# Cross-attention and ternary FFN: a third plane of keys, fewer TensorE waits, maxima written in place, another order of small transfers

## What is computed

```python
x = x + xattn(layernorm(x), ctx, mask)        # x 32x56x128, ctx 32x1500x128, 16 heads of 8
#   scores = q k^T / sqrt(8), -1e9 where mask == 0, softmax over 1500 keys, times v, times Wo + bo
x = x + ffn(layernorm(x))                      # 128 -> 512 -> 128
#   weights ternary, rows quantised to 8 bits before each product, exact gelu between
```

## Time and profile before

| | |
|---|---|
| median of 3 runs | 975.32 us (970.74 to 975.33) |
| the profiled execution | 970.35 us, its span 968.6 us |
| granted TensorE clock, mean | 0.959 of full speed |

### The profile page before, as it was taken

One profiled execution on the slowest core, in us unless ns is written; L12 is line 12 of the kernel. 1 busy time (PEld: TensorE's weight loads), 2 busy tenths in 40 slices (PEclk: granted clock), 3 DMA queues, 4 the chain that ended last, 5 costly groups with the idle time before them and its releaser, 6 DMA issues.

```text
span 968.6 us, 35820 instructions
## 1 busy us (share of the span) xinstructions
PE 859.6 (89%) x12492; PEld 655.2 (68%) x12492; DVE 758.8 (78%) x2597; ACT 707.5 (73%) x1272; POOL 252.2 (26%) x262
## 2 busy tenths in 40 slices
PE   3667989999898989999898999899898989989893
PEld 2344767767676767767686777677676767767672
DVE  4578579888787979888787979788686978878754
ACT  3434658879697868879697878779596877969562
POOL 8220242222222222222222222222222222312200
PEclk9677999999999999999999999999899999999997
DMA  5540223333322333333332333333323333340100
GB/s 139 117 119 18 63 51 86 89 92 83 100 72 75 82 87 84 90 92 83 94 78 73 81 90 86 82 91 83 97 56 82 76 89 91 85 104 24 36 3 6
DMA packets 79099, 75.79 MB, mean 78 GB/s; under 512 B 10240, under 2 KB 75248, under 8 KB 78960
## 3 DMA queue, kind: packets, MB, share of 16 engines
q1 hardware_dynamic: 77167, 72.78, 29.5%
q10 hardware_dynamic: 1793, 0.83, 0.3%
HBM read 47.97 MB, written 0.92 MB: 50 GB/s over the span
## 4 chain that ended last, share of the span: by engine, by line
PE 70%; issue 12%; ACT 6%; DVE 4%; SPq 4%; DMA 2%; POOL 2%; ACTq 0%; POOLq 0%; DVEq 0%
PE ps_p L885 18%; PE ps_v L929 12%; PE ps_p L867 9%; PE ps_p L812 8%; PE ps_p L808 8%; PE ps_p L893 7%; PE ps_p L805 4%; SPq L456 2%; ACT L690 2%; ACT L723 2%; DMA ctx_sb<-in_ctx_dram 1%; DVE max_junk L1165 1%; ACT probs L723 1%; PE ps_p L836 1%; PE ps_p L832 1%
## 5 line engine op out<-in xcount | busy, mean ns | idle before, releaser
L1165 DVE CUSTOM_DVE_ANT_0 max_junk<-ps_p,mask_bias 120x500 bf16<-120x500 f32 x768 | 483.2, 674 | 71.8 <-PE ps_p L867 53.7
L723 ACT ACTIVATE probs<-ps_p 125x448 f32<-125x448 f32 x768 | 355.3, 558 | 77.1 <-PE ps_p L893 73.3
L885 PE MATMUL ps_p<-qry_hi,keys 64*125 64x224 f32 x1536 | 208.0, 291 | 6.6 <-ACT probs L723 0.6
L634 POOL TENSOR_TENSOR k_lo<-k_full,keys 128x500 fp32r<-128x500 f32 x96 | 125.7, 1316 | 319.5 <-ACT keys L713 255.6
L885 PE MATMUL ps_p<-qry_lo,keys 64*125 64x224 f32 x1536 | 192.9, 271 | 0.0
L885 PEld LDWEIGHTS ps_p<-qry_hi,keys 64*125 64x125 f32 x1536 | 150.4, 186 | 61.9 <-ACT probs L723 29.2
L867 PE MATMUL ps_p<-keys,qry_hi 64*120 64x500 f32 x768 | 161.2, 438 | 13.1 <-DMA keys<-k_lo 5.9
L929 PEld LDWEIGHTS ps_v<-probs,vals 125*32 125x32 f32 x6144 | 145.1, 110 | 23.3 <-issue 12.8
L929 PE MATMUL ps_v<-probs,vals 125*32 125x112 f32 x6144 | 160.6, 260 | 0.2 <-ACT probs L723 0.2
L893 PE MATMUL ps_p<-own_query,mask_bias 57*125 57x448 f32 x768 | 147.0, 373 | 9.3 <-DMA own_query<-shift 9.2
L885 PEld LDWEIGHTS ps_p<-qry_lo,keys 64*125 64x125 f32 x1536 | 151.1, 187 | 3.2
(11 more groups left out here) (124 smaller groups left out, 804.3 us busy)
## 6 DMA issues: line engine op xcount, KB each, us to landing
keys<-k_lo SPq DMA_DIRECT2D x384, 62.5 KB, 2.0
ctx_sb<-in_ctx_dram SPq DMA_DIRECT2D x31, 750.0 KB
mask_sb<-in_mask_Bx1xSxS_ik_dram SPq DMA_DIRECT2D x64, 328.1 KB
own_query<-shift SPq DMA_DIRECT2D x64, 1.8 KB
out_dram<-x_rows SPq DMA_DIRECT2D x16, 56.0 KB, 1.6
ctx_sb<-in_ctx_dram ACTq DMA_DIRECT2D x1, 750.0 KB
x_rows<-in_x_dram SPq DMA_DIRECT2D x1, 672.0 KB, 11.0
w_sb<-in_L_ffn_w_dram SPq DMA_DIRECT2D x2, 256.0 KB, 8.4
```

Of the source, the lines that this page charges most:

```text
L634: pool.tensor_tensor(k_lo[:, (p + n) % 2, :], k_full[:, (p + n) % 2, :], keys[:, p, 0, at].bitcast(F32), ALU.subtract)\
L723: act.activation(probs[:, (c + NG * p) % NP, h], ps_p[0:KC, BANK[how]["S", c, h], 0:HC], ACT.Exp)\
L885: pe.matmul(score_bank(c, h, how)[:, heads, :], keys[rows, p, g, at], query[rows], start=(g == 0 and part == 0), stop=False, skip_group_ch ...
L1165: dve.tensor_tensor_reduce(max_junk[0:MROWS, BANK[how][slot], :], ps_p[0:MROWS, BANK[how][slot], 0:SEG], mask_bias[0:MROWS, p, s * SEG:(s ...
```

## The change

1. `keys` has a third plane. Plane 0 is left as it is made, the high parts of all eight heads of a half in their natural rows; planes 1 and 2 are the stacked ones of before. ScalarE writes planes 0 and 1, and a new GpSimd copy of 128x500 per segment writes plane 2 from plane 0; the low parts go into planes 1 and 2. Of the four transfers of a segment, the two into plane 2 wait for that copy. The maxima read planes 1 and 2.
2. In `products`, the queries' low parts meet plane 0 in one matmul of 448 columns per half; the high parts meet planes 1 and 2 in two of 224 each. Eight matmuls become six, with the same number of columns in all.
3. TensorE leaves out a wait where an earlier one of the same step on the same semaphore asked for as much (`wait_once`; a slot's second bank is waited for first), and some waits whose condition another wait implies. The wait on `wo_rows` moves ahead of the steps.
4. The maxima's unused sums are written over the bank that they are read from, 32-bit words in PSUM; `max_junk` goes.
5. `vals` shares the ones between two neighbouring pairs of heads (values, ones, values); the rows of `wo_rows` and `den_of_row` follow.
6. In odd steps SyncE places the shift row ahead of segment 1.

```diff
-        keys = sb("keys", [D, 2, 2, SK], F32R)
+        keys = sb("keys", [D, 2, 3, SK], F32R)
         k_lo = sb("k_lo", [D, 2, SEG], F32R)
         mask_bias = sb("mask_bias", [128, 2, SK], F32R)
-        vals = sb("vals", [KC, 2, NC, NV, 2, VH])
...
-        max_junk = sb("max_junk", [128, NBANK, SEG], BF16)
...
-            def place_low(bt, n):
+            def place_keys(bt, n):
 
                 b, k, p = bt
                 made = NSEG * b + n + 1
                 at = slice(n * SEG, (n + 1) * SEG)
-                sp.wait_ge(k_lo_ready, made if isinstance(b, int) else sp.snap(made))
-                for h in range(2):
-                    for g in range(2):
+                made = made if isinstance(b, int) else sp.snap(made)
+                sp.wait_ge(k_lo_ready, made)
+                for g in range(2):
+                    if g == 1:
+                        sp.wait_ge(keys_copied, made)
+                    for h in range(2):
                         src, dst = SLOT * h + GR * g, SLOT * h + GR * (1 - g)
-                        sp.dma_start(keys[dst:dst + GR, p, g, at].bitcast(F32), k_lo[src:src + GR, (p + n) % 2, :].bitcast(F32))\
-                            .then_inc(k_lo_placed[p][n], 16)
+                        sp.dma_start(keys[dst:dst + GR, p, 1 + g, at].bitcast(F32),
+                                     k_lo[src:src + GR, (p + n) % 2, :].bitcast(F32)).then_inc(keys_placed[p][n], 16)
 
             def store(bt):
...
                     if loop or b > 1:
                         store(bt)
                     if loop or b + 2 < B:
-                        place_low(later(bt, 2), 0)
-                    if loop or b + 2 < B:
-                        place_low(later(bt, 2), 1)
+                        place_keys(later(bt, 2), 0)
                     if loop or b + 1 < B:
                         place_shift(later(bt, 1))
                     if loop or b + 2 < B:
-                        place_low(later(bt, 2), 2)
+                        place_keys(later(bt, 2), 1)
+                    if loop or b + 2 < B:
+                        place_keys(later(bt, 2), 2)
 
...
                 if n == 2:
-                    pool.wait_ge(k_lo_placed[p][0], 64 * (k + 1))
+                    pool.wait_ge(keys_placed[p][0], 64 * (k + 1))
                 else:
-                    wait(pool, k_lo_placed[1 - p][n + 1], 64 * (k + p))
+                    wait(pool, keys_placed[1 - p][n + 1], 64 * (k + p))
                 pool.tensor_tensor(k_lo[:, (p + n) % 2, :], k_full[:, (p + n) % 2, :],
                                    keys[:, p, 0, at].bitcast(F32), ALU.subtract)\
                     .then_inc(k_lo_ready, 1)
+                pool.tensor_copy(keys[:, p, 2, at], keys[:, p, 0, at].bitcast(F32)).then_inc(keys_copied, 1)
...
-                    act.activation(vals[:, p, 4 * n:4 * n + 4, :, 0, :].rearrange("p c v r -> p (c v) r"),
-                                   bank[0:KC, :].rearrange("p (v r) -> p v r", r=VH), ACT.Copy)\
+                    act.activation(vals[:, p, 4 * n:4 * n + 4, :, 0::2, :].rearrange("p c v a r -> p (c v) a r"),
+                                   bank[0:KC, :].rearrange("p (v a r) -> p v a r", a=2, r=VH), ACT.Copy)\
...
-                act.activation(keys[:, p, :, at],
+                act.activation(keys[:, p, 0:2, at],
...
+            waited = {}
+
+            def wait_once(semaphore, count, st):
+
+                level = count((st[2], 0, st[2]))
+                if level > waited.get(semaphore.name, -10 ** 9):
+                    waited[semaphore.name] = level
+                    wait(pe, semaphore, count(st))
+
+            def wait_bank(slot, how, st):
+                last, ago = before(how, slot)
+                if last is not None:
+                    wait_once(left_bank[last[0]], lambda bt: number(last, later(bt, -ago)), st)
+
+            def wait_banks(kind, n, how, st):
+
+                for h in (1, 0):
+                    wait_bank((kind, n, h), how, st)
 
...
                 if kind == "D":
                     pe.wait_ge(pv_taken, b + 1)
-                    pe.wait_ge(halves_known, 1)
+                    if isinstance(b, int):
+                        pe.wait_ge(halves_known, 1)
                 if kind == "B":
                     pe.wait_ge(wo_scaled, 1)
                 if kind == "O":
                     pe.wait_ge(attn_ready, 2 * (t + 1))
-                    pe.wait_ge(wo_rows_loaded, 16 * N_WO_ROWS)
...
                 if r == 0:
-                    pe.wait_ge(k_lo_placed[p][s], 64 * (k + 1))
-                for h in range(2):
-                    wait_bank_free(pe, ("M", n, h), how, st)
+                    pe.wait_ge(keys_placed[p][s], 64 * (k + 1))
+                wait_banks("M", n, how, st)
                 for h in range(2):
                     rows = slice(SLOT * h, SLOT * (h + 1))
                     pe.matmul(ps_p[0:MROWS, BANK[how]["M", n, h], 0:SEG],
                               qry_hi[rows, p, 2 * r:2 * r + 2, :].rearrange("p a q -> p (a q)")[:, 0:MROWS],
-                              keys[rows, p, r // 2, s * SEG:(s + 1) * SEG], start=True, stop=True)\
+                              keys[rows, p, 1 + r // 2, s * SEG:(s + 1) * SEG], start=True, stop=True)\
                         .then_inc(bank_full[BANK[how]["M", n, h]], 1)
...
                 at = slice(c * KC, (c + 1) * KC)
+                for h in range(2):
+                    rows = slice(SLOT * h, SLOT * (h + 1))
+                    pe.matmul(score_bank(c, h, how), keys[rows, p, 0, at], qry_lo[rows, p, :, :], start=True, stop=False,
+                              skip_group_check=True)
                 for g in range(2):
                     heads = slice(GH * g, GH * (g + 1))
-                    for part, query in enumerate((qry_hi[:, p, heads, 0:SQ], qry_lo[:, p, heads, :])):
-                        for h in range(2):
-                            rows = slice(SLOT * h, SLOT * (h + 1))
-                            pe.matmul(score_bank(c, h, how)[:, heads, :], keys[rows, p, g, at], query[rows],
-                                      start=(g == 0 and part == 0), stop=False,
-                                      skip_group_check=True)
+                    for h in range(2):
+                        rows = slice(SLOT * h, SLOT * (h + 1))
+                        pe.matmul(score_bank(c, h, how)[:, heads, :], keys[rows, p, 1 + g, at],
+                                  qry_hi[rows, p, heads, 0:SQ], start=False, stop=False, skip_group_check=True)
 
             def shifts(bt, c, how):
...
                 if c == 0:
                     pe.wait_ge(q_step, 4 * (b + 1))
-                if c % NG == 0:
-                    pe.wait_ge(k_lo_placed[p][c // NG], 64 * (k + 1))
-                for h in range(2):
-                    wait_bank_free(pe, ("S", c, h), how, bt)
+                wait_banks("S", c, how, bt)
                 products(bt, c, how)
...
-                if c % NG == 0:
-                    pe.wait_ge(mask_biased, NSEG * b + c // NG + 1)
                 shifts(bt, c, how).then_inc(scores_ready, 1)
+
+            def with_ones(p, c, t):
+
+                return vals[:, p, c, t // 2, t % 2:t % 2 + 2, :].rearrange("p a r -> p (a r)")
 
             def values(bt, n):
 
                 b, k, p = bt
                 if n == 0:
                     wait(pe, pv_taken, b)
-                pe.wait_ge(vals_ready, NSEG * b + n + 1)
-                pe.wait_ge(exp_done, 2 * (NC * b + NG * (n + 1)))
+                wait_once(exp_done, lambda at: 2 * (NC * at[0] + NG * (n + 1)), bt)
...
 
             step(batch(-1, 0), "open")
             step(batch(-1, 1), "lead")
+            pe.wait_ge(wo_rows_loaded, 16 * N_WO_ROWS)
             steps(pe, step)
             step(batch(B // 2, 0), "tail")
...
-                dve.tensor_tensor_reduce(max_junk[0:MROWS, BANK[how][slot], :],
+                dve.tensor_tensor_reduce(ps_p[0:MROWS, BANK[how][slot], 0:SEG],
                                          ps_p[0:MROWS, BANK[how][slot], 0:SEG],
                                          mask_bias[0:MROWS, p, s * SEG:(s + 1) * SEG].bitcast(F32), 1.0, LOWEST,
                                          ALU.add, ALU.max, seg_max[0:MROWS, 4 * h + r, s:s + 1])\
```

More of the change, by code:

```diff
@@ L309, in xattn_ffn @@
         k_hi_ready = sem("k_hi_ready")
+        keys_copied = sem("keys_copied")
         k_lo_ready = sem("k_lo_ready")
-        k_lo_placed = [[sem(f"k_lo_placed{p}_{n}") for n in range(NSEG)] for p in range(2)]
+        keys_placed = [[sem(f"keys_placed{p}_{n}") for n in range(NSEG)] for p in range(2)]
         vals_ready = sem("vals_ready")
@@ L517, in _ @@
             for n in range(NSEG):
-                place_low(batch(0, 0), n)
+                place_keys(batch(0, 0), n)
             sp.dma_start(wo_sb[:], wo).then_inc(wo_loaded, 16)
@@ L526, in _ @@
                     at = VH * (4 * t + g)
```

(13 more changed lines are left out.)

3 lines of the change are left out of this document (2 added, 1 removed).

## The result

The kernel after takes 935.90 us (median of 4, 931.15 to 937.74), the kernel before 975.33 (median of 4): ratio 0.9591, 95% interval 0.9536 to 0.9645. That is 39 us less, where 7 were forecast, and outside the range; it is the time of the rival that had a chance of 0.05.

A forecast was written before the change was run, and what follows sets the result against it. It took TensorE and VectorE to bound the even half, TensorE and, around the Gelu, ScalarE the odd. Terms -2 + 0 - 4 + 1 + 0 = -5 us against 970.35 gave about 965; median forecast 968, range 955 to 988.

The forecast's parts named there:

- the rival that had a chance of 0.05: TensorE's 2.8 us stall at nearly every iteration's end disappears with the shorter loop body; about 936 us, chance 0.05.
- The stall at the iteration's end goes: Rival: TensorE's loop is shorter by 48 matmuls, weight loads and waits, so its stall vanishes; about 936 us, chance 0.05.
- The maxima's write: VectorE's maxima writing 32-bit words into PSUM: taken as 0, upper bound +28 us in the even half.
- the rival: Slower by the maxima's write: VectorE's pitch in the even stretch rises 0.03 to 0.074 us; 979 to 996, chance 0.20.
- The argument from overlap: VectorE's next maximum starts before the former's write has ended (0.60 against 0.674 us), so a later end need not move the pitch.
- the mark of this rival: Sign of the slower case: a pitch of VectorE's maxima over 0.62 us, with a longer even half.
- The order of transfers: Shift row issued ahead of the second four key transfers at an odd batch's end: -4 us (-1 to -5.4).
- Products: TensorE's four pairs of 224-column matmuls per key chunk become two of 224 and one of 448: -2 us (0 to -8).
- waits: Some 38 of about 185 TensorE waits per iteration go; a met wait costs nothing: 0 us (0 to -3).
- copy: 96 new GpSimd copies of 128x500, 0.6 us each, could show as contention: +1 us (0 to +5).
- The contention that the prediction feared: GpSimd's copies slow VectorE, as a scaling took 0.62 us beside a low-key subtraction, 0.33 otherwise; 0.3 us once per iteration.
- the small forecast: The whole kernel gains a little by the edits' summed terms, -5 us; new median 968 us, chance 0.50.

The follow-up runs named there:

- b_order: The kernel before with only the new order of transfers (shift row ahead of the second four key transfers): 963.61 us, ratio 0.9923.
- a_sbmax: The kernel after with the maxima's outputs of the loop's batches back in SBUF as bf16: 921.55 us, ratio 0.9459.
- b_pad_order: The kernel before with 130 idle instructions at the start of TensorE's program and the new order of transfers: 926.83 us, ratio 0.9525.
- a_pad186: The kernel after with 186 idle instructions at the start of TensorE's program: 997.96 us, ratio to before 1.0257.
- b_pad130: The kernel before with only 130 idle instructions put at the start of TensorE's program: 944.03 us, ratio 0.9711.
- b_pad230: The kernel before with only 230 idle instructions put at the start of TensorE's program: 984.48 us, ratio 1.0137.
- a_waits: The kernel after with TensorE's covered waits put back, 25 instructions more in the loop: 931.95 us, ratio 0.9549.

## Why the prediction was wrong

**The step that failed** is the rival "The stall at the iteration's end goes" and the sentence that set its chance: "nothing shows that length is its cause". Its time, 936, was right, in part by luck (it took 13 x 2.5 = 32.5 us for the stalls, where the fetching made 28.8 in the loop and some 3 us of the gain lie outside it); its chance of 0.05 was not. The page did show something: 127 instruction packets for a program of 20, nine in a stalled iteration and one in the iteration behind the missing stall. The prediction saw that iteration and took it only as proof that the stall "can be missing". It also named length as the one candidate, where place counts as much: the kernel of 1,697 instructions runs without the stall in one place, that of 1,577 with it in another. In this change, by the blocks of the table, either would have been enough (an estimate, not run): the old loop at the new place would span 7.20 to 13.82, the new one at the old place 7.68 to 13.84, seven blocks each. The packets, set beside the compiled loop's length and place, would, as I judge it, have raised that chance well above 0.05, and with it the low end of the range, which at 955 left the case out.

**The maxima's write** was the next error: taken at 0, with 28 as upper bound and 20% for the rival. It costs 0.78 us an iteration, 10 us in the 13 stretches and 14 in the medians (935.90 against 921.55, which were not run side by side), so a third to a half of the bound. The argument from overlap failed: the write's end isn't in the pitch, but the pitch rose all the same, 0.60 to 0.64, past the 0.62 that the prediction had named as the mark of this rival. The rule drawn on, of 60 ns access on SBUF and 125 on PSUM (the Trainium skill, "Perfetto Trace Analysis", Optimizing Scalar/DVE Operations), had the sign right; its estimate of 65 ns each is above the 31 ns of duration and 40 ns of pitch measured here.

**The order of transfers** was understood and under-sized. Beside the stall it was put at -4 and measured at about -8 (b_order, interval 4 to 11). Without the stall, which the prediction itself named as the cover, it is worth 0.98 to 1.30 us an iteration, 13 to 17 us. In after two waits for the shift row are left, 4.0 us in the start-up and 1.08 in the last pair. The two that the prediction expected to go, 0.99 and 2.39 us, are gone; the one in the last pair was 1.06 us in before. The waits of after, then the last one in before and in after:

```profile
PE ps_p L918 <- DMA own_query<-shift: 5.1, 2, 4.0
```

```profile
933.66 0.47 PE L893 MATMUL ps_p<-own_query,mask_bias 57*125 57x448 f32 x2 [1.06 <-DMA own_query<-shift]
```

```profile
894.49 0.47 PE L918 MATMUL ps_p<-own_query,mask_bias 57*125 57x448 f32 x2 [1.08 <-DMA own_query<-shift]
```

**Products, waits, copy** held: -2 forecast for the products, 0.10 us an iteration or some 1.5 us measured; 0 and 0 for the waits; and GpSimd's copies last 605 ns each where 0.6 us was taken, with at most 0.05 us an iteration left for them. The contention that the prediction feared is there, but off the path: VectorE is busy 0.25 us longer per iteration with the copies (45.26 in a_sbmax, 45.01 in b_pad_order), near the 0.3 named. In before the scaling it named lasts 286 ns in the last two of its 16 runs, where no low-key subtraction runs beside it, and 647 to 679 in the other 14, where one does (the shortest, middle and longest in ns):

```profile
L1034 DVE TENSOR_SCALAR w_sb<-w_sb,row_stat x16: 286/666/679, 165.5 to 959.5; 112x128 f32<-112x128 f32 x16
```

The copies of after:

```profile
L642 POOL CAST keys<-keys 128x500 fp32r<-128x500 f32 x96 | 58.0, 605 | 0.0
```

The edits alone, -7.4 us in the loop, are near the -5 of the sum, but by two errors of opposite sign (in the 13 stretches the order gave 13 to 17 where 4 were taken, the maxima cost 10 where 0 was). And the small forecast was small for a wrong reason: the largest term was not what an edit computes, but where the loop came to lie.

## What to carry to other kernels

Read the instruction queue's line of the page against the size of the program: many more packets than the program has blocks mean that a loop is fetched again, and then any edit that lengthens, shortens or moves the code can cost or gain more than what it computes. When a stall is removed, ask which wait it had covered, since an edit worth little beside the stall may be worth most of the rest. Before a DVE output is moved into PSUM to save SBUF, look whether dead start-up tensors have room: here they did, and the version with them is the fastest, 921.55 us.

## What was not expected of the hardware

Idle instructions at the start, which compute nothing and move the loop, changed the time from 972 to 944 (130 of them) and 984 us (230) in one kernel and from 936 to 998 in the other. A loop fetched again cost 2 us an iteration in before and 8.6 in a_pad186, where the stall was longer (4.17 against 2.8 us, with two packets in it) and TensorE ran at the lower of its two clocks for a while behind it. And idle instructions are not free: 186 delayed the first loop branch by 13.6 us, though 130 delayed it by 4.2. Most of this can be read from TensorE's first matmul, in before, b_pad130, a_pad186 and b_pad230:

```profile
12.87 2.73 PE L805 MATMUL ps_p<-ident,ctx_sb 125*128 125x125 f32 x12 [12.87 <-DMA ctx_sb<-in_ctx_dram]
```

```profile
16.88 2.73 PE L807 MATMUL ps_p<-ident,ctx_sb 125*128 125x125 f32 x12 [16.88 <-issue]
```

```profile
22.94 2.73 PE L831 MATMUL ps_p<-ident,ctx_sb 125*128 125x125 f32 x12 [22.94 <-issue]
```

```profile
27.89 2.73 PE L807 MATMUL ps_p<-ident,ctx_sb 125*128 125x125 f32 x12 [27.89 <-issue]
```

Without idle instructions it waits for its data until 12.87 us. From 130 to 186 to 230 of them it starts 0.11 us later for each one more, so by this pitch some 94 fit into the time in which TensorE has nothing to do (an estimate from these four rows), and the rest delay everything behind them. The same kind of instruction cost nothing in the loop (a_waits), where matmuls are at work.
